# The last group's residual in a decoder layer: added by VectorE, not by TensorE

## The reference

```
xe = x[:, :16, :]                      # the first 16 tokens of each sequence: one expert a token
y = _layernorm(xe, g_e, b_e)
h = gelu(einsum('bnd,ndh->bnh', y, W1_e) + b1_e)
out_e = einsum('bnh,nhk->bnk', h, W2_e) + b2_e
xr = x[:, 16:, :]                      # the other 112 tokens: one shared pair of weights
yr = _layernorm(xr, g_s, b_s)
out_s = gelu(yr @ W1_s + b1_s) @ W2_s + b2_s
return concatenate([out_e, out_s], axis=1)
...
x = _layernorm(x + _L0_ffn_ref(x, ...))    # no gain, no bias
```

## Time and profile before

| What | Value |
|---|---|
| Median of 3 runs | 499.02 us (498.51 to 500.15) |
| Profiled execution, its own time | 498.26 us |
| Its span in the trace | 496.3 us |
| PE busy | 473.1 us, 95% |
| DVE busy | 381.6 us, 77% |
| ACT busy | 367.2 us, 74% |
| POOL busy | 261.5 us, 53% |
| Mean granted TensorE clock | 0.988 |

### The profile page before, as it was taken

The page is one execution under the profiler, slowest core; times in us unless marked ns, Lnnn a source line. Parts: engine busy times, 40 slices in busy tenths (PEclk is TensorE's granted clock), DMA queues, the critical chain, the costliest instruction groups (busy, mean ns, idle before and its releaser), DMA issues.

```text
span 496.3 us, 14185 instructions
## 1 busy us (share of the span) xinstructions
PE 473.1 (95%) x4668; PEld 435.2 (88%) x4668; DVE 381.6 (77%) x1831; ACT 367.2 (74%) x1392; POOL 261.5 (53%) x379
## 2 busy tenths in 40 slices
PE   7778999999999999999999999999999999999993
PEld 7778889999999999999999999999999998798872
DVE  3678778898888977887777777777777777647874
ACT  3547887868677788877778887777777776754864
POOL 3455357665565755555545455544444455534553
PEclk9899999999999999999999999999999999999996
DMA  8750000000000005000000000000000000600004
GB/s 230 232 212 1 1 3 1 2 2 2 1 3 1 3 3 126 1 3 1 3 1 2 2 2 1 2 3 1 4 1 3 1 2 2 171 22 1 6 7 106
DMA packets 15688, 14.58 MB, mean 29 GB/s; under 512 B 2816, under 2 KB 13056, under 8 KB 15488
## 3 DMA queue, kind: packets, MB, share of 16 engines
q1 hardware_dynamic: 14048, 13.20, 9.0%
q10 hardware_dynamic: 1568, 0.47, 0.4%
HBM read 12.23 MB, written 1.44 MB: 28 GB/s over the span
## 4 chain that ended last, share of the span: by engine, by line
PE 74%; DVE 12%; ACT 6%; issue 3%; DMA 2%; POOL 2%; SPq 0%; DVEq 0%; ACTq 0%
PE late_bank L595 11%; PE late_bank L547 10%; PE late_bank L564 10%; PE late_bank L579 10%; PE late_bank L72 9%; PE late_bank L74 8%; PE late_bank L73 8%; ACT P L843 3%; DVE P L1119 3%; PE late_bank L290 2%; PE late_bank L604 1%; PE late_bank L624 1%; PE late_bank L626 1%; PE late_bank L625 1%; DMA tap_rows<-in_short_wT 1%
## 5 line engine op out<-in xcount | busy, mean ns | idle before, releaser
L843 ACT ACTIVATE P<-P,at_negmax 128x128 f32<-128x128 f32 x512 | 198.9, 396 | 78.8 <-DVE at_negmax L1119 78.8
L1529 POOL TENSOR_TENSOR P<-P,at_inv 128x512 f32<-128x512 f32 x128 | 136.6, 1078 | 121.9 <-DVE at_inv L1129 121.9
L1145 DVE COPY at_PT<-late_bank 128x512 f32<-128x512 f32 x128 | 87.6, 687 | 35.4 <-PE late_bank L547 35.3
L1119 DVE CUSTOM_DVE_ANT_0 P<-late_bank,maskb 128x128 f32<-128x128 f32 x512 | 110.5, 287 | 2.4 <-PE late_bank L564 2.4
L843 ACT ACTIVATION_READ_ACCUMULATOR P<-P,at_negmax 128x1 f32 x512 | 100.2, 196 | 0.0
L547 PE MATMUL late_bank<-ident,P 128*128 128x128 f32 x512 | 76.3, 273 | 2.0 <-DVE at_negmax L1119 1.0
L547 PEld LDWEIGHTS late_bank<-ident,P 128*128 128x128 f32 x512 | 59.7, 140 | 8.4 <-issue 3.9
L564 PE MATMUL late_bank<-at_k,at_q 64*128 64x128 f32 x1024 | 65.8, 278 | 0.9 <-DVE at_k L1137 0.9
L564 PEld LDWEIGHTS late_bank<-at_k,at_q 64*128 64x128 f32 x1024 | 59.7, 188 | 4.8 <-issue 1.2
L579 PE MATMUL late_bank<-at_PT,V 128*64 128x128 f32 x1024 | 63.0, 276 | 0.0
L579 PEld LDWEIGHTS late_bank<-at_PT,V 128*64 128x64 f32 x1024 | 55.2, 137 | 3.9
(11 more groups left out here) (199 smaller groups left out, 1068.7 us busy)
## 6 DMA issues: line engine op xcount, KB each, us to landing
ctxT_raw<-in_ctxT SPq DMA_DIRECT2D x1, 1024.0 KB, 8.3
out<-xres SPq DMA_DIRECT2D x4, 224.0 KB, 2.5
x<-in_xT SPq DMA_DIRECT2D x1, 768.0 KB, 10.4
xres<-in_x SPq DMA_DIRECT2D x1, 768.0 KB, 14.4
tap_rows<-in_short_wT SPq DMA_DIRECT2D x3, 192.0 KB, 5.1
sa_wq_raw<-in_sa_wq SPq DMA_DIRECT2D x1, 512.0 KB, 7.0
sa_wk_raw<-in_sa_wk SPq DMA_DIRECT2D x1, 512.0 KB, 9.3
sa_wv_raw<-in_sa_wv SPq DMA_DIRECT2D x1, 512.0 KB, 10.8
```

The costliest lines, as they stand in the source:

```text
L843: last = nc.scalar.activation(P[:, n % 2, h, :], P[:, n % 2, h, :], ACT.Exp, scale=-1.0, bias=negmax[:, n % 2, h:h + 1], accum_out=total[: ...
L1119: last = nc.vector.tensor_tensor_reduce(P[:, n % 2, h, :], score_bank(h), k.maskb[:, cols(n)], scale=1.0, scalar=3.0e38, op0=ALU.add, op1= ...
L1145: nc.vector.tensor_copy(PT[:, HQ * g:HQ * g + HQ, :], banks[T_BANK[g % 2]][:].rearrange("p (h l) -> p h l", h=HQ)).then_inc(pt_ok, 1)
L1529: nc.gpsimd.tensor_tensor(tile, tile, inv[:, n % 2, HQ * g:HQ * g + HQ].unsqueeze(2).to_broadcast([128, HQ, 128]), ALU.mult).then_inc(norm ...
```

## The change

The residual of group 3 is no longer added on TensorE (`add_x4(3)` is gone) but on VectorE (`output_sum(3)` is new). `SUMMED` becomes the list of groups that are summed on VectorE, now 0, 1 and 3. Everything of group 3 that read the bank now reads `res`: the statistics, VectorE's half of the normalisation and ScalarE's half.

```
-        SUMMED = 2
+        SUMMED = (0, 1, 3)
...
             experts_w2()
-            add_x4(3)
             shared_w2(3)
...
-                    source = res[:, s] if g < SUMMED else banks[W2_BANK[g]][:, b * 128:(b + 1) * 128]
+                    source = res[:, s] if g in SUMMED else banks[W2_BANK[g]][:, b * 128:(b + 1) * 128]
...
-                    last = nc.scalar.activation(res[:, s], banks[W2_BANK[LAST]][:, b * 128:(b + 1) * 128], ACT.Identity,
+                    last = nc.scalar.activation(res[:, s], res[:, s], ACT.Identity,
                                                 bias=shift3[:, OUT, s:s + 1], scale=rstd3[:, OUT, s:s + 1])
...
-                if g < SUMMED:
-                    vec.wait_ge(out_res, g + 1)
+                if g in SUMMED:
+                    vec.wait_ge(out_res, SUMMED.index(g) + 1)
                     moments(g, 2, res[:, group(g)])
...
-                    last = nc.vector.tensor_scalar(res[:, s], banks[W2_BANK[LAST]][:, b * 128:(b + 1) * 128],
+                    last = nc.vector.tensor_scalar(res[:, s], res[:, s],
                                                    mv3[:, 2, s, 0:1], rstd3[:, OUT, s:s + 1], ALU.subtract, ALU.mult)
...
             experts_sums()
+            output_sum(3)
             output_statistics(3)
```

## The result

The changed kernel takes 499.55 us (median of 22 runs, 498.10 to 501.80) against 498.19 us (22 runs) of the kernel before on the same chips: ratio 1.0025, interval 1.0014 to 1.0036. Measured again beside the experiments, in 12 runs against 35, it is 1.0011 (0.9993 to 1.0029). The first measurement makes it slower by 0.1 to 0.4%; the second agrees in sign, but its interval also holds no change. The forecast was 499.6 us and +0.13%.

What follows compares the result with a forecast made beforehand. Bound: the chain of waits through VectorE's late work at group 3's statistics, with 0.40 us of TensorE slack. Terms 0.72 - 0.02 - 0.13 + 0.07 = +0.64 us on 499.02 gave 499.6 us (+0.13%), range 498.4 to 501.0 us.

Steps and rivals of the forecast that it cites:

- The chain: Waits from the experts' residual through VectorE's experts' sum and group 3's statistics to ScalarE's end and the store: +0.64 us.
- the sum: Term for VectorE's added `output_sum(3)`, between the experts' variance and group 3's statistics, hidden by nothing: +0.72 us.
- the two halves of the normalisation: Group 3's normalisation read from SBUF instead of the bank: VectorE's half -0.13 us, ScalarE's half +0.07 us.
- step 1: Removing TensorE's `add_x4(3)` is worth 0; group 3's products end at 487.0 us, or 488.05 at 1.2 GHz, before 489.05.
- Rival 1: VectorE's SBUF reads in `last_output` hold up GpSimd's shift, delaying ScalarE: +1.08 us in sum, 500.1 us; chance 0.11.
- the rule that the prediction brings under this rival: A two-port VectorE operation and a GpSimd one exclude each other from a shared SBUF port pair for a whole instruction.
- Rival 2: TensorE was the bound in timed runs, as the experts' residual lands earlier: cost only +0.12 us, 499.1 us; chance 0.11.
- Rivals 3 and 4: Rival 3: the end of TensorE's program sets the time, so 1.65 us go, 497.4 us, chance 0.02; beside rival 4.
- rival 4: Group 3's products on TensorE at the low clock become the bound: +2.5 us, 501.6 us; chance 0.02.
- the sum itself: Adding the terms, 0.72 - 0.02 - 0.13 + 0.07 = +0.64 us, onto the 499.02 us median of three runs.
- Term 5: VectorE's `last_output` reading SBUF instead of the bank: 0.60 us for two operations against 0.73, so -0.13 us.
- the other estimate in the prediction: From the Trainium skill's fixed costs and double SBUF rate: -0.26 us for VectorE's two `last_output` operations, sum +0.51 us.

Runs made afterwards that it cites:

- e3: Changed kernel, with TensorE's product of the residual with the identity still made, into a bank nothing reads; 1.0012 of the kernel before.
- e4: The changed kernel as it is, timed and traced again beside the experiments; 1.0011 of the kernel before.
- e2: Kernel before plus VectorE's sum of group 3; TensorE's product kept, statistics and normalisation still read the bank; 1.0011 of the kernel before.
- e9: e2 with group 3's statistics reading the result tile in SBUF, both normalisation halves still reading the bank; 1.0013 of the kernel before.
- e10: e2 with both halves of the normalisation reading the result tile in SBUF, statistics still reading the bank; 1.0007 of the kernel before.
- e1: Kernel before without TensorE's product of group 3's residual with the identity, VectorE unchanged; 0.9998 of the kernel before.
- e11: Changed kernel without ScalarE's wait for VectorE's half of the last normalisation; 1.0016 of the kernel before.
- e12: e11 with VectorE normalising three of the last four sequences and ScalarE one; 0.9991 of the kernel before.
- e5: Kernel before plus eight idle 128x512 products on TensorE, whose results nothing reads; 1.0013 of the kernel before.
- e6: Changed kernel plus eight idle 128x512 products on TensorE, whose results nothing reads; 1.0023 of the kernel before.

## Why the prediction was right, and where it was short

The mechanism was the one forecast. That the time itself was met to 0.05 us is luck, as said under the result.

**The chain, right.** The tail grew by 0.65 us in the change's profile (0.66 in e3 and e4), forecast +0.64. Term by term: the sum +0.72 (7.13 against 6.41, e2), the statistics -0.01 (e9; forecast -0.02), the two halves of the normalisation -0.05 (e10; forecast -0.13 + 0.07).

**TensorE's product, worth nothing: right in the traces of the change, e1 and e3**, and in line with their times, 0.9998 and 1.0012 against 1.0011, which alone could not show it. The bound of step 1 for a low clock (an end by 488.1 us) did not hold in the profile: the products ended at 487.48 + 1.77 = 489.25 us, since they started only at 487.48 us. I had let the clock slow these products but not what comes ahead of them. It cost nothing there, because the same clock made VectorE late by 0.69 us: 0.5 us were left to the addition's start at 489.74 us.

**Rival 1** did not happen: the shift took 0.20 us in the change, e10, e11 and e12 alike, and in the change ScalarE waited for VectorE:

```profile
493.31 0.20 POOL L1639 TENSOR_TENSOR ffshift<-ffminus,ffrstd 128x4 f32<-128x4 f32 x1
```

It lies across VectorE's first operation on `xres` (from 493.10 us, 0.34 us long) and starts 0.27 us behind the minus mean's start, as it did beside the bank reads the earlier trace rows. So nothing here shows that one of the two shuts the other out for a whole instruction, the rule that the prediction brings under this rival; the 0.26 us beside L1328 stay unexplained.

**Rival 2**'s mechanism was seen in e2, by another lever than I gave: the prediction took the end of the experts' products at 486.01 us as fixed. How often it happens in the kernel before is open: its one trace shows 0.40 us of slack. **Rivals 3 and 4** did not occur, though the half clock of rival 4 did; it hit the experts' products and moved the whole tail.

**The step that fell short is the sum itself, which left out the time outside the span.** It added the differences along the chain inside the span and put the result on the device time, with nothing for what lies outside, and gave no reason. Device time less span is a steady number for each kernel, with a standard error of 0.02 us or less. It is 2.02 to 2.03 us for the kernel before (2.04 and 2.02 in e1 and e5) and 2.18 to 2.19 us for the changed kernel in both its measurements, so it adds 0.16 us. The change by its parts is then 0.65 + 0.16 = 0.81 us, 0.16%, inside both intervals. The forecast's 0.13% was within the second and just under the first.

**The base was wrong as well.** The prediction saw that the profiled execution (498.26 us) lay 0.76 us under the median of three runs, and chose the median. The 22 runs have their median at 498.19 us: the profiled execution was the ordinary one, and the median of three was high.

**Term 5** was sized rightly by the rows: VectorE's half from SBUF took 0.13 us less in e10 and in the change (0.60 against 0.73), not 0.26 us less, which the other estimate in the prediction gave.

What makes up the rest between 0.81 us and the first measurement's 1.26 us (means of 22 runs) is not shown. The standard error of that difference is 0.27 us, from two standard deviations of 0.9 us, so it need not have a cause.

## What to carry to other kernels

Where one engine's work at the end is taken to another, ask which of the two is late there, not which is busier: TensorE at 95% had slack at that place, and the addition came on the engine that had none. A move of the source from PSUM to SBUF was worth 0.06 us here. More came of looking again at the order around it: with the two engines' turn gone and the shares rebalanced, the 0.65 us in the chain came back (e12), though how much of that needs the move was not tried. Slack is to be computed with the clock low through the whole stretch ahead of it, not for the moved instructions alone.

## What the runs showed that was not expected

- TensorE's granted clock fell to half in every one of the 14 traces while TensorE was still at its last work, starting between 481 and 486 us, for 3.4 us in eight of them and 6.8 us in six, at a place that differed between executions with the same work ahead of it. In 7 of them it was also low somewhere between 8 and 25 us. Two stretches of the start, before and after the change:

```profile
16.00:24.00 8.00, 6.82 (x40) 6.37 (x41) 4.98 (x14) 3.94 (x9) 3.73 (x8) 0.79 0.64 166
```
```profile
16.00:24.00 8.00, 7.10 (x37) 6.83 (x38) 5.16 (x14) 4.03 (x9) 3.46 (x8) 0.61 0.74 178
```

  In the seven without it TensorE's last transposes (L667) start at 476.8 to 477.6 us, in the seven with it at 476.9 to 480.2 us. The low clock does not explain that alone: the changed kernel's two executions start them at 477.94 and 480.18 us (e4), and both had the low clock for 6.8 us in all, one from 17 to 25 us, e4 at 8 to 12 and 18 to 22 us. So a part of the scatter of about 1.1 us, in which a 0.65 us effect must be found, has a cause that stays open.
- The time outside the span takes one of three values by kernel: 1.90 to 1.92 us (e2, e10, e12), 2.02 to 2.04 (before, e1, e5), 2.17 to 2.19 (the change, e3, e4, e6 to e9, e11). The theories of e9 and e10 on it were half borne out: the statistics' source moved it (2.17), the outputs' did not (1.92), but e12 reads its statistics from SBUF too and has 1.90. Its cause is open.
